# The opening of a fused attention kernel rebuilt: squares on arrival, the first x turned by TensorE, products of zeros first, all calls of the opening in a new order

## The reference

```python
def attn(x):                       # Wq, Wk, Wv, Wo are 512 x 512
    Q, K, V = x @ Wq.T + bq, x @ Wk.T + bk, x @ Wv.T + bv   # each split into 16 heads of 32
    s = einsum('nqhd,nkhd->nhqk', Q, K) / sqrt(32)          # here q and k run over the 16 heads of ONE token
    out = einsum('nhql,nlhd->nqhd', softmax(s), V)
    return out.reshape(8, 2048, 512) @ Wo.T + bo
x = x + layernorm(attn(layernorm(x)))
x = x + layernorm(ffn(layernorm(x)))    # ffn: a residual block that ends in layernorm(...) * ln_g + ln_b
```

## Time and profile before

| | us |
|---|---|
| median of three runs | 1621.95 |
| the profiled execution | 1621.66 |
| its span, first to last instruction | 1619.9 |
| what lies around the span | 1.76 |
| PE (TensorE matmul) busy | 1578.2 (97%) |
| POOL (GpSimd) busy | 1387.8 (86%) |
| DVE (VectorE) busy | 1356.4 (84%) |
| ACT (ScalarE) busy | 962.2 (59%) |

### The profile page before, as it was taken

The page is one execution under the profiler, slowest core; times in us unless marked ns, Lnnn a source line. Parts: engine busy times, 40 slices in busy tenths (PEclk is TensorE's granted clock), DMA queues, the critical chain, the costliest instruction groups (busy, mean ns, idle before and its releaser), DMA issues.

```text
span 1619.9 us, 59515 instructions
## 1 busy us (share of the span) xinstructions
PE 1578.2 (97%) x22566; PEld 918.3 (57%) x22566; DVE 1356.4 (84%) x2476; ACT 962.2 (59%) x2009; POOL 1387.8 (86%) x1429
## 2 busy tenths in 40 slices
PE   8899999999999999999999999999999999999993
PEld 3555555555555555555555555555555555555551
DVE  7678888888888888888888888888888888888887
ACT  5455665665665665665665665665665665665654
POOL 4668988988988988988988988988988988888867
PEclk9999999999999999999999999999999999999996
DMA  6756766766766767766767766766767767667652
GB/s 227 187 136 183 203 161 194 200 161 197 200 161 197 200 158 200 199 159 200 199 158 201 197 160 201 198 159 202 195 159 204 193 162 204 193 160 205 160 146 77
DMA packets 388653, 293.72 MB, mean 181 GB/s; under 512 B 296854, under 2 KB 296854, under 8 KB 388380
## 3 DMA queue, kind: packets, MB, share of 16 engines
q1 hardware_dynamic: 345936, 223.54, 51.8%
q10 hardware_dynamic: 42444, 66.37, 13.1%
HBM read 155.46 MB, written 67.24 MB: 137 GB/s over the span
## 4 chain that ended last, share of the span: by engine, by line
PE 93%; POOL 3%; DVE 2%; ACT 1%; issue 1%; DMA 0%; ACTq 0%; POOLq 0%; SPq 0%; DVEq 0%
PE ps_k L1321 8%; PE ps_q L1321 7%; PE ps_v L1321 7%; PE ps_y L1420 7%; PE ps_q L1327 7%; PE ps_k L1327 7%; PE ps_v L1327 7%; PE ps_y L1422 7%; PE ps_q L1336 7%; PE ps_k L1336 7%; PE ps_v L1336 7%; PE ps_y L1425 6%; PE ps_s L1375 6%; PE ps_o L1397 5%; DMA x_t<-in_xt 0%
## 5 line engine op out<-in xcount | busy, mean ns | idle before, releaser
L1115 ACT ACTIVATE q_sb<-ps_q,qk_back 128x512 f32<-128x512 f32 x127 | 87.6, 690 | 360.4 <-PE ps_q L1336 358.4
L486 POOL TENSOR_TENSOR o_sb<-o_sb,x 128x512 f32<-128x512 f32 x122 | 153.6, 1278 | 95.8 <-ACT o_sb L1066 95.6
L451 POOL TENSOR_TENSOR x_t<-x_t,mr_row 128x512 f32<-128x512 f32 x126 | 195.9, 1555 | 7.4 <-DMA mr_row<-x_d 5.2
L458 POOL TENSOR_TENSOR x_t<-x_t,mr_row 128x512 f32<-128x512 f32 x126 | 195.5, 1552 | 0.5
L739 DVE SCALAR_TENSOR_TENSOR x<-ps_y,y_back,bo_row 128x512 f32<-128x512 f32 x125 | 93.8, 750 | 99.4 <-PE ps_y L1425 99.3
L464 POOL TENSOR_TENSOR xT_lo<-x_t,xT_hi 128x512 f16<-128x512 f32 x127 | 163.2, 1285 | 6.3 <-ACT xT L1083 6.2
L1321 PE MATMUL ps_v<-wv_hi,xT_hi 128*128 128x512 f32 x508 | 162.5, 441 | 1.4 <-ACT v_tok L1122 1.4
L728 DVE STREAM_TRANSPOSE qT<-q_sb 128x512 f32<-128x512 f32 x128 | 134.5, 1051 | 34.0 <-ACT q_sb L1115 34.0
L474 POOL TENSOR_TENSOR x<-x,res 128x512 f32<-128x512 f32 x124 | 159.2, 1284 | 3.5 <-ACT x L1066 3.5
L1321 PE MATMUL ps_q<-wq_hi,xT_hi 128*128 128x512 f32 x508 | 161.9, 440 | 0.0
L1321 PE MATMUL ps_k<-wk_hi,xT_hi 128*128 128x512 f32 x508 | 158.1, 433 | 3.4 <-POOL xT_lo L464 1.7
(11 more groups left out here) (215 smaller groups left out, 3593.2 us busy)
## 6 DMA issues: line engine op xcount, KB each, us to landing
x_in<-in_xa SPq DMA_DIRECT2D x64, 512.0 KB, 6.4
x_t<-in_xt SPq DMA_DIRECT2D x64, 512.0 KB, 8.5
k_bd<-kT SPq DMA_DIRECT2D x512, 64.0 KB, 2.9
v_d<-v_tok ACTq DMA_DIRECT2D x128, 256.0 KB, 2.4
v_key<-v_d SPq DMA_DIRECT2D x128, 256.0 KB, 4.4
res<-in_xr SPq DMA_DIRECT2D x64, 512.0 KB, 5.5
p_bd<-pT ACTq DMA_DIRECT2D x500, 64.0 KB, 2.6
out<-o_sb SPq DMA_DIRECT2D x62, 512.0 KB, 7.3
```

Source lines behind the costliest of these rows:

```text
L451: nc.gpsimd.tensor_tensor(x_t[v % 2][:, j, :, :], x_t[v % 2][:, j, :, :], mr_row[v % 2][:, :, 0, j].unsqueeze(1).to_broadcast([P, EC, P]), ...
L458: nc.gpsimd.tensor_tensor(x_t[v % 2][:, j, :, :], x_t[v % 2][:, j, :, :], mr_row[v % 2][:, :, 1, j].unsqueeze(1).to_broadcast([P, EC, P]), ...
L486: nc.gpsimd.tensor_tensor(o_sb[:, v % 2, j, :], o_sb[:, v % 2, j, :], x1[:, v % 3, j, :], ALU.add).then_inc(out_done, 1)
```

## The change

What it does, in the order of the program:

1. The first rows and the biases of k, q and v are packed into one input `w_row` and come in two transfers.
2. `squares` no longer waits for `even_out`. It takes the raw half as it lands; `squares_row` adds 512 times the squares of the first row, and the squares of the bias; `totals` adds four sums and not two. `even_out` now waits for the squares of its half, since both use the buffer. `put_bias` moves to GpSimd.
3. Pair 0 of x is normalised as it was loaded, by token, with one VectorE instruction per tile (`first_norm`), then turned by TensorE against the identity (`turn`, four products per tile). `x_high`, `x_half` and the rest (`first_lows`, both on VectorE) read the bank. The transposed copy of pair 0 is not loaded.
4. `warm` multiplies zeros: nine products of 128 x 128 by 128 x 512 in float16 at the very start, four more ahead of `turn(1)`.
5. Pair 1 of x gets its rows through DRAM like the later pairs.
6. The second halves of q and v come first (`taken`), one `half` of q and one of v go to ScalarE, in tile 0 the products with `xT_lo` come before those with `w_lo`, `totals("q")` stands before `keys(0)`, `keys(2)` behind the scores of tiles 0 and 1.
7. The no-operations ahead of the loop go from 34 to 238.

The loop and the tail stay as they are on TensorE.

```diff
+        taken = {"k": (0, 1), "q": (1, 0), "v": (1, 0), "o": (0, 1)}
+        def nth(k, i):
+            return 2 * order.index(k) + taken[k].index(i) + 1
...
             sp.dma_start(x_in[0][:, :, :], xa[0]).then_inc(x_first, DMA)
             load_half("k", wk, 0)
-            load_xt(0)
             load_half("k", wk, 1)
+            load_x(1)
+            load_half("q", wq, 1)
             load_half("q", wq, 0)
...
+            nc.vector.memset(oT_hi[1][:, :, :].bitcast(F32), 0.0).then_inc(own_done, 1)
+            nc.vector.memset(w_sq[:, :, :], 0.0).then_inc(own_done, 1)
...
             def first_norm(j):
-                dve.wait_ge(rows_ready, 2)
-                dve.wait_ge(first_centred, 2 * j + 1)
-                nc.vector.tensor_tensor(x_t[0][:, j, :, :], x_t[0][:, j, :, :],
-                                        ps_s[:, 1, j * P:(j + 1) * P].unsqueeze(1).to_broadcast([P, EC, P]), ALU.mult
-                                        ).then_inc(first_centred, 1)
+                dve.wait_ge(root_done["X"], 1)
+                nc.vector.tensor_scalar(x_t[0][:, j, :, :].rearrange("p e n -> p (e n)"), x_in[0][:, j, :], mr[0][:, 0, j:j + 1],
+                                        mr[0][:, 1, j:j + 1], ALU.subtract, ALU.mult).then_inc(first_centred, 1)
+            def first_lows(j):
+                dve.wait_ge(xhi_done, 2 * j + 2)
+                nc.vector.tensor_tensor(xT_lo[j][:, :, :], xT_bank[j].rearrange("p (e n) -> p e n", e=EC),
+                                        xT_hi[j][:, :, :].bitcast(F32), ALU.subtract).then_inc(first_low, 1)
...
             def even_out(k, i):
                 dve.wait_ge(w0_spread, order.index(k) + 1)
                 dve.wait_ge(w_loaded[k][i], DMA)
+                dve.wait_ge(w_squared, squared[k, i])
...
             def squares(k, i, hi):
                 n = order.index(k)
-                if k == "o":
-                    act.wait_ge(w_loaded[k][i], DMA)
-                else:
-                    act.wait_ge(w_even, 2 * n + i + 1)
-                    act.wait_ge(b_put, n + 1)
+                act.wait_ge(w_loaded[k][i], DMA)
+            def squares_row(k):
+                n, (w_junk, b_junk) = order.index(k), row_junk[k]
+                act.wait_ge(row_loaded[k], DMA)
+                act.wait_ge(own_done, 2)
+                nc.scalar.activation(w_junk, w_0[k], ACT.Square, scale=float(E) ** 0.5, accum_out=w_sq[0:1, n, 2:3]
+                                     ).then_inc(w_squared, 1)
+                nc.scalar.activation(b_junk, w_b[k], ACT.Square, accum_out=w_sq[0:1, n, 3:4]).then_inc(w_squared, 1)
...
+            def turn(j):
+                pe.wait_ge(first_centred, j + 1)
+                for e in range(EC):
+                    mm = nc.tensor.matmul(xT_bank[j][:, e * P:(e + 1) * P], x_t[0][:, j, e, :], ident[:, :], start=True, stop=True)
                 mm.then_inc(rows_ready, 1)
+            def warm(count):
+                still = oT_hi[1][:, :, :].rearrange("p a n -> p (a n)").bitcast(F16)
+                for _ in range(count):
+                    nc.tensor.matmul(ps_k[:, :], still[:, 0:P], still[:, 0:E], start=True, stop=True)
...
+            pe.wait_ge(own_done, 1)
+            warm(9)
             pe.wait_ge(ones_set, 1)
             spread("k")
...
+            turn(0)
             spread("q")
+            totals("k")
             spread("v")
-            totals("k")
+            warm(4)
+            turn(1)
+            totals("q")
             keys(0)
-            totals("q")
             keys(1)
+            totals("v")
             queries(0)
...
             queries(1)
+            spare(30)
             values(0)
-            spare(7)
+            spare(30)
             values(1)
-            spare(7)
-            keys(2)
             scores(0)
             scores(1)
+            spare(30)
+            keys(2)
```

More of the change, by code:

```diff
@@ L144, in fused @@
         rows_ready = sem("rows_ready")
-        rows_put = sem("rows_put")
         first_centred = sem("first_centred")
@@ L468, in half, with put_bias @@
                 pool.wait_ge(w_scaled, 2 * order.index(k) + 1)
+                if k != "o":
+                    pool.wait_ge(w_even, nth(k, i))
+                    if i == 0:
+                        pool.wait_ge(b_put, order.index(k) + 1)
                 nc.gpsimd.tensor_scalar(w_16[:, halves[i], :], raw[k][:, halves[i], :], scale_of(k), 1.0, ALU.mult, ALU.mult
                                         ).then_inc(w_half, 1)
+            def put_bias(k):
+                pool.wait_ge(row_loaded[k], DMA)
+                pool.wait_ge(w_even, nth(k, 0))
+                nc.gpsimd.tensor_copy(raw[k][0:1, 0, :], w_b[k]).then_inc(b_put, 1)
             def x1_add(v, j):
@@ L544, in _ @@
             nc.gpsimd.memset(p_bd[:, :, :, :], 0.0).then_inc(p_zeroed, 1)
+            put_bias("k")
             half("k", 0, wk_16)
+            x_root(1)
             half("k", 1, wk_16)
-            x_low(1)
-            x_root(1)
-            half("q", 0, wq_16)
+            put_bias("q")
             half("q", 1, wq_16)
-            half("v", 0, wv_16)
             x_centre(2)
+            half("v", 1, wv_16)
+            put_bias("v")
+            x_root(2)
             x_norm(2)
@@ L556, in _ @@
             x_norm(3)
-            x_root(2)
+            x_centre(4)
             x_low(3)
+            x_norm(4)
+            normalise(0)
+            x_root(3)
+            x_centre(5)
+            normalise(1)
             half("o", 0, wo_16)
-            normalise(0)
-            normalise(1)
+            x_low(4)
             half("o", 1, wo_16)
-            x_centre(4)
-            x_norm(4)
-            x_root(3)
-            x_low(4)
-            x_centre(5)
             x_norm(5)
@@ L1240, in _ @@
             exponent(0)
+            cast("o", 0, wo_hi)
+            q_in(2)
             exponent(1)
-            q_in(2)
             probs_half_out(0)
-            probs_half_out(1)
-            cast("o", 0, wo_hi)
-            cast("o", 1, wo_hi)
             v_in(2)
-            q_in(3)
             x_high(4)
             x_half(4)
-            v_in(3)
+            q_in(3)
+            probs_half_out(1)
+            cast("o", 1, wo_hi)
             x_high(5)
             x_half(5)
+            v_in(3)
             for p in range(2, NV - 1):
@@ L1430, in spare @@
                     nc.tensor.nop(hint='pad', nofuse=True)
-            def rows(v, part, to):
-                for i, q in enumerate(part):
-                    mm = nc.tensor.matmul(to[:, i * P:(i + 1) * P], mr[v][:, q // 2, q % 2:q % 2 + 1].to_broadcast([P, P]),
-                                          ident[:, :], start=True, stop=True)
+            def turn(j):
+                pe.wait_ge(first_centred, j + 1)
+                for e in range(EC):
+                    mm = nc.tensor.matmul(xT_bank[j][:, e * P:(e + 1) * P], x_t[0][:, j, e, :], ident[:, :], start=True, stop=True)
                 mm.then_inc(rows_ready, 1)
```

309 lines of the change are left out of this document (159 added, 150 removed).

## The result

The changed kernel takes 1627.3 us (median of seven runs, 1624.38 to 1630.03), the kernel before 1621.95. The ratio is 1.0034 with a 95% interval of 1.0024 to 1.0045: slower by 0.34%. A second set of ten runs gave 1625.77 and 1.0020 [1.0011, 1.0030]. The forecast was 1614.9, in a range of 1610.5 to 1619.0: wrong in sign, and outside its range.

A forecast was written before the change was run, and what follows sets the result against it. TensorE, busy 97%, was taken to bound the kernel, so only an earlier loop start helps: 1621.66 - 5.4 (opening) - 1.7 (stall in mixed(0)) = 1614.6, median 0.3 above, 1614.9 us; range 1610.5 to 1619.0.

The forecast's parts named there:

- To the scale of k: Opening: at the low clock level sums of k end at 13.5, scale at 13.9 us against 14.3; 0.4 gained.
- The rule of the Trainium skill: Two-port VectorE and GpSimd instructions exclude each other: first_norm begins at 8.55, chain 1.7 us longer, time 1616.6.
- Zeros raise the clock early: Rival, opening: the nine zeros products bring TensorE's high clock early, 3.1 us more gain, 1611.8; chance 0.27.
- keys(0) at 21.4, scale of q at 23.1: Opening: TensorE is ready for keys(0) at 21.4 us; VectorE's queue, 1.7 per `low`, gives q's scale at 23.1.
- Rows of pair 1 at 27: Opening: rows read back through DRAM from near 22, taking 4.3 us, land about 27; x_centre(2) done by 30.
- 204 more no-operations at nothing: Ahead of the loop: hidden while matmuls run, priced at nothing; uncovered, a fraction of a microsecond for each 30.
- The 1.70 in `mixed(0)` goes: Behind the loop's start: the wait for instructions ("issue") disappears, gaining 1.7 us; bounds 0 and 1.7.
- Loop's first scores at 57.4: End of the opening: scores(0) at 39.4, then projections and sums; loop starts at 57.4, not 62.77, gaining 5.4 us.
- low level and stall stay: Rival, opening and mixed(0): TensorE at half speed until keys(1), instruction fetch still late; 1617.6 us; chance 0.21.
- slower: Rival: pair 1's late rows hold GpSimd's x_centre(2), deciding from a landing at 30; landing at 40 gives 1625; chance 0.06.

The follow-up runs named there:

- lean kernel: Changed kernel with pair 1's rows read early, loop's start reordered, zeros out and 8 no-operations ahead of the loop: 1617.39 us, 0.9968 of the kernel before.
- the memset early: Lean kernel with GpSimd's memset of p_bd ahead of x_root(0), so late rows, no-operations and memset are all mended: 1616.6 us, 0.9963 of the kernel before.
- half a block off: Lean kernel with 128 more no-operations behind the spreading of k's row, where TensorE waits for first_norm: 1810.65 us, 1.1160 of the kernel before.

## Why the prediction was wrong, step by step

- *To the scale of k.* The order of events was right. `first_norm` was priced at 0.52 and took 1.91 beside the memset, so the sums of k start at 12.97 and not 11.5. The rule of the Trainium skill, "SBUF — State Buffer", section "Who interferes with whom", was left out of the forecast, since `even_out` showed nothing; that is another form, and the rule held. With the memset out of the way the lean kernel's loop starts 1.6 us earlier.
- *Zeros raise the clock early* (0.27). The nine at the start did so in some profiled executions and not in others, and it never lasted: behind the wait for `first_norm` turn(0) takes 2.04 either way. With the four ahead of `turn(1)` keys(0) is at the high level in some (1.18 for four products) and not in others (2.05); in the five changed kernels without zeros it never is. TensorE gains 1.7 and 1.9 us by it at queries(0) in the two pairs of profiles, and nothing of it is in the medians.
- *keys(0) at 21.4, scale of q at 23.1.* Measured 20.89 and 22.6. A `low` beside nothing took 1.28, not 1.7.
- *Rows of pair 1 at 27.* The first step that failed. The reading was issued at 23.68 and not near 22, and took 8.0 us and not 4.3: the 4.3 was of a transfer with an empty queue ahead of it, this one had 2.3 MB. The prediction counted those as 6 us in the rival, and left them out of the forecast. Cost: 4 us at the loop's start, and 2 to 4.5 in the medians, by the edit and by which set of the changed kernel it is held against.
- *204 more no-operations at nothing.* The second step that failed. The prediction said that they are hidden while matmuls run, and a fraction of a microsecond for each 30 otherwise. But 30 take 2.2 us, and it did not look at the places where TensorE's sequencer is less far ahead than that. Behind queries(0), values(0) and the scores they lay open: 0.72, 0.75, 1.98. Out, with the zeros, they give 4.8 us. The pace could be read in the kernel before, where each 14 of the loop take 1.0 us from the first to the last:

```profile
L1430 PEldq NOP  x14: 13/13/13, 74.5 to 75.5; - x14
```

- *The 1.70 in `mixed(0)` goes.* It did, but 1.34 and 0.90 for `k_bd` and `p_bd` took its place; in the lean kernel it comes back as 1.62 one iteration later, with the memset early as 1.60 and 0.62. This term is to be struck.
- *Loop's first scores at 57.4.* With the three mended it is 56.93, but not by the chain that the forecast followed. That chain went over ScalarE and VectorE to `q_turn(1)` and gave 39.4 for the scores of tile 0; there `q_turn(1)` ends at 38.0, and TensorE, without a gap from 7.7 us on, comes to the scores at 38.80. The two paths were nearly equal, and that the number fits is in part luck. The time is then 1616.6, 1.7 above the forecast, although the loop starts 0.5 earlier: the waits behind its start are 2.8 us, where the forecast had none.
- The rival *low level and stall stay* named neither cause. The *slower* rival named the first and was given 0.06: for a landing counted at 28 beside the turning point of 30, both of them estimates, that was far too little (31.7 and about 28.6 by the traces). The range did not contain the two failures together.

## What to carry over

A transfer that is moved behind others is priced by its queue at that moment, not by its time in a quiet one; and the engine that waits for it holds everything behind it, so ask for the cheapest order in which nothing urgent stands behind the wait (here: three lines swapped on GpSimd, or one line on SP, 4 us). No-operations are free only where the sequencer is ahead: count 74 ns each against its lead, by the distance of their starts and not by the duration in their records, and when a list must keep its place against blocks of 256, go down to the nearer multiple by removing work that doesn't pay before filling up to the next. And several small losses in series behind an expected gain want a range that holds them all at once.

## What the runs showed of the hardware

- A two-operation tensor_scalar of 128x512 float32 on VectorE takes 546 ns alone and 1910 beside a GpSimd memset of 128x2048 float32; the subtraction of `even_out` (tensor_tensor with a bank of PSUM) took 1.22 us beside the same memset in the kernel before.
- A no-operation holds TensorE's list for 72 to 76 ns, though its record says 13: 30 take 2.2 us, 90 take 6.5, 128 take 9.3.
- Half a block (128 instructions) decides whether the loop runs without a wait for instructions from its third iteration on, or has one of 1.6 to 2.7 us in nearly every iteration: 1617.4 or 1810.7 us.
- TensorE's level fell to the low one behind waits of 2.27 to 2.45 us at the loop's start in three kernels, and stayed behind one of 2.37 in a fourth; behind 1.34 and 1.43 it stayed. Behind the "issue" of 2.0 us ahead of keys(2) it fell in two kernels and stayed in four. In the kernel that is half a block off it fell in sixteen iterations of 61, behind waits as long (2.44) as in others where it stayed. In the opening it rose at 20 us in one execution of the changed kernel and at 25 in the other.
